# Graph network on one core: the row that VectorE's source one-hots compare with moves from SBUF to PSUM

## The chip, the cores and the metric

One core of a Trainium2 chip runs the whole network as one program. The metric is the device time of one execution in microseconds; the median of three runs before the change is 2574.71 us. The profile is of one further execution on the same kind of core. Its instructions span 2204.9 us.

## The reference, cut to what matters

`x` holds 3125 nodes of 256 features, and there are 53125 edges, sorted by target. Four layers follow each other, each added to `x` after a layer norm: a graph attention, a top-1 mixture of experts, a graph convolution and a top-2 mixture of experts. The change lies in the attention's stage of the edges, and in the counts that the later graph convolution needs:

```
Q, K  = (x @ Wq), (x @ Wk)                        # 8 heads of 32
score = (Q[src] * K[tgt]).sum(-1) * scale + edge_attr @ We
...
out_deg = maximum(segment_sum(ones, src), 1)      # in the second graph layer
msg     = (t1[src] + feat[src] * feat[dst] @ W2) / (sqrt(out_deg[src]) * sqrt(out_deg[dst]))
```

`out_deg`, the number of edges that leave each node, is computed in the stage of the edges, as a by-product: for each tile of 128 edges a product of two one-hots adds to a table of 125 by 25 counts.

## The kernel before

The edges lie as 420 tiles of up to 128 edges, one edge to a partition, in 84 groups of G = 5 tiles. A source node s is written as hi * 125 + lo, with lo in 0..124 and hi in 0..24. The stage of the edges is one block of the program in which every engine runs its own loop over the 84 groups, tied to the others by semaphores only. Its engines do the following for group n, in their own order.

- GpSimd (line 808) issues five gathers, one a tile: 128 rows of `q_rows` in device memory, named by the numbers that `src_t` holds in SBUF, into one of eight buffers of `qr`. It waits until VectorE has freed the buffer of eight groups ago (`s_free`).
- VectorE makes half of the key one-hots of group n+1 (line 978, two instructions). It then waits for `s_ohu` and makes the source one-hots of group n: `oh_lo` (line 1004, 5 x 125 elements a partition) and `oh_hi` (line 1006, 5 x 25), each a compare of a row of numbers with the edges' `lo` or `hi`. The row is `iota_row`, 0..124, in SBUF. It waits for the gathered rows, multiplies them by the expanded keys in PSUM (line 1011, three instructions, `qr` by `psK`) and reduces the products to the dot products (line 1014), which frees the buffer.
- ScalarE makes the other half of the key one-hots (lines 829 and 833), fetches the turned attributes (843, 844) and keeps the scores (854).
- TensorE expands the keys to rows (line 906, 20 matmuls into the three banks of `psK`, each bank once VectorE has freed it), turns the attributes of group n+1 (891), makes the edge scores of group n (918) and adds the counts of group n (line 933, five matmuls into the first 25 columns of `psC`). The counts' bank is opened by a matmul of zeros (877) and read once at the end (1017).
- SyncE loads the local key numbers (764) and the edge attributes (752 to 755).

`s_ohu` counts the groups whose counts TensorE has made. Before the change it starts at GI = 4, so the one-hots of group n wait for the counts of group n-4, the last user of their buffer.

Of the kernel before, what the change touches and what calls it, by code (L numbers as in the profile page):

```python
# [16 lines left out]
P = 125  # L17
T = N_NODES // P
G = 5
NG = T // G  # L20
E = 128
# [5 lines left out]
GI = 4  # L27
# [44 lines left out]
def build(nc, x, src, dst, edge_attr_64, L0_gnn_Wq, L0_gnn_Wk, L0_gnn_Wv, L0_gnn_We, L0_gnn_Wo, L0_gnn_bo,  # L72
# [4 lines left out]
    def sb(ctx, name, shape, dt=F32):  # L77
        return ctx.enter_context(nc.sbuf_tensor(name, shape, dt))
# [4 lines left out]
    def ps(ctx, name, shape, dt=F32):  # L83
        return ctx.enter_context(nc.psum_tensor(name, shape, dt))
# [10 lines left out]
    with top:  # L95
# [22 lines left out]
        iota_row = sb(top, "iota_row", [E, P])  # L118
# [110 lines left out]
        def sem1(name):  # L229
            sems1.append(nc.alloc_semaphore(name=name))  # L230
            return sems1[-1]
# [4 lines left out]
        with ExitStack() as st:  # L236
# [331 lines left out]
            def _(v):  # L568
# [45 lines left out]
                def places():  # L614
# [83 lines left out]
        s_oh, s_ohu, s_cnt, s_webz, s_cntz = (sem1(n) for n in ("onehots_made", "onehots_used", "counts_done", "we_zeroed",  # L698
                                                       "zero_lhs"))
        s_kt, s_kabs, s_kta, s_kx, s_kfree, s_dT, s_dk, s_dst1 = (sem1(n) for n in (  # L700
            "k_onehots", "k_distances", "k_onehots_act", "k_expanded", "k_banks_free", "dots_turned", "dots_kept", "dots_stored"))
        with ExitStack() as st:
# [14 lines left out]
            oh_lo = sb(st, "oh_lo", [E, GI, G, P], BF16)  # L717
            oh_hi = sb(st, "oh_hi", [E, GI, G, T], BF16)
            zb = sb(st, "zb", [P, P], BF16)
            psE = ps(st, "psE1", [128, 2, 512])  # L720
            psS = ps(st, "psS1", [128, 2, 512])
            psC = ps(st, "psC1", [128, 512])
            psK = ps(st, "psK1", [128, 3, 512])
            block = st.enter_context(nc.Block(no_gpsimd_drain=True))
            eav = edge_attr_64[0:FULL * J].rearrange("(p j) f -> p (j f)", p=FULL)
            ear = edge_attr_64[FULL * J:N_EDGES].rearrange("(p j) f -> p (j f)", p=1)
# [145 lines left out]
            @block.tensor  # L872
            def _(pe):
                pe.sem_inc(s_ead, GI)
                pe.sem_inc(s_ohu, GI)
                pe.wait_ge(s_cntz, 1)
                nc.tensor.matmul(psC[0:P, 0:T], zb[:], zb[:, 0:T], start=True, stop=False, skip_group_check=True)
                pe.wait_ge(s_webd, 32)
                def named_bases(i, g):

# [77 lines left out]
                with pe.Fori(begin, EITER - 1) as i:  # L958
# [3 lines left out]
                                 skip_group_check=True).then_inc(s_cnt, 1)  # L962
# [9 lines left out]
            @block.vector  # L972
            def _(v):
                def k_onehots(slot, k_slot, turn):

                    v.wait_ge(s_loc[slot], 16 * (turn + 1))
                    for c in range(CD):
                        last = nc.vector.tensor_scalar(oh_k[:, k_slot, c, :], loc[:, slot, :], k_at[:, c:c + 1], None, ALU.is_equal)
                    last.then_inc(s_kt, 1)

                nc.vector.memset(we2[:], 0.0).then_inc(s_webz, 1)
                nc.vector.memset(ea[:, 0, :], 0.0).then_inc(s_eaz, 1)
                nc.vector.memset(zb[:], 0.0).then_inc(s_cntz, 1)
                nc.vector.memset(ea[:, 1:GI, :], 0.0).then_inc(s_eaz, 1)
                for n in range(2):
                    last = nc.vector.tensor_scalar(part_of[:, n:n + 1], rank_p[:, 0:1], float((n + 1) * R), -float(R), ALU.is_ge, ALU.mult)
                dve_order.link(v, last)
                for n in range(2):
                    dve_order.link(v, nc.vector.tensor_scalar(k_at[:], rank_p[:] if n == 0 else k_at[:], part_of[:, n:n + 1], None, ALU.add))

                dve_order.link(v, nc.vector.tensor_copy(src_f[:], src_i[:]))
                dve_order.link(v, nc.vector.tensor_scalar(lo[:], src_f[:], -float(P // 2), 1.0 / P, ALU.add, ALU.mult))
                dve_order.link(v, nc.vector.tensor_scalar(hi[:], lo[:], MAGIC, None, ALU.add))
                dve_order.link(v, nc.vector.tensor_scalar(hi[:], hi[:], MAGIC, None, ALU.subtract))
                dve_order.link(v, nc.vector.scalar_tensor_tensor(lo[:], hi[:], -float(P), src_f[:], ALU.mult, ALU.add))
                dve_order.link(v, nc.vector.tensor_scalar(k_neg[:], k_at[:], -1.0, None, ALU.mult))
                v.sem_inc(s_kt, GI)
                v.sem_inc(s_kfree, 3)
                k_onehots(0, K_SLOT[0], 0)
                for n in range(NK):  # L1000
                    g, row, at = n % GI, qr[:, n % GQ], slice(n * G, (n + 1) * G)
                    k_onehots((n + 1) % GI, K_SLOT[(n + 1) % GI], (n + 1) // GI)
                    v.wait_ge(s_ohu, n + 1)
                    nc.vector.tensor_tensor(oh_lo[:, g], iota_row[:].unsqueeze(1).to_broadcast([E, G, P]),
                                            lo[:, at].unsqueeze(2).to_broadcast([E, G, P]), ALU.is_equal)
                    nc.vector.tensor_tensor(oh_hi[:, g], iota_row[:, 0:T].unsqueeze(1).to_broadcast([E, G, T]),
                                            hi[:, at].unsqueeze(2).to_broadcast([E, G, T]), ALU.is_equal).then_inc(s_oh, 1)
                    v.wait_ge(s_got[n % GQ], G * 16 * (n // GQ + 1))
                    for m, (a, b) in enumerate(BANKS):
                        v.wait_ge(s_kx, n * 3 + m + 1)  # L1010
                        nc.vector.tensor_tensor(row[:, a:b].rearrange("p u d -> p (u d)"), row[:, a:b].rearrange("p u d -> p (u d)"),  # L1011
                                                psK[:, m, 0:(b - a) * D], ALU.mult).then_inc(s_kfree, 1)
                    v.wait_ge(s_kfree, n * 3 + 6)
                    nc.vector.tensor_reduce(dots[:, :, at].rearrange("p h u -> p u h"),  # L1014
                                            row.rearrange("p u (h d) -> p u h d", h=H), AX.X, ALU.add).then_inc(s_free, 1)
                v.wait_ge(s_cnt, 1)
                dve_order.link(v, nc.vector.tensor_copy(counts[:, 0, :], psC[0:P, 0:T]))

                dve_order.link(v, nc.vector.tensor_scalar(counts[0:1, 0, 0:1], counts[0:1, 0, 0:1], -float(PADS), None, ALU.add))
# [1245 lines left out]
        with ExitStack() as st:  # L2265
# [64 lines left out]
            def _(v):  # L2330
                link = lambda ins: dve_order.link(v, ins)

                def rest(m):

                    _, whole, part = piece(m)
                    v.wait_ge(s_hi7, m + 1)
                    link(nc.vector.tensor_tensor(whole, whole, part[0], ALU.subtract))
                    v.sem_inc(s_rest7, 1)

                def low_part(m):  # L2340

                    _, whole, part = piece(m)
                    v.wait_ge(s_mid7, m + 1)
                    nc.vector.tensor_tensor(part[2], whole, part[1], ALU.subtract).then_inc(s_lo7, 1)
# [56 lines left out]
            def _(act):  # L2401
# [10 lines left out]
                def middle_part(m):  # L2412

                    _, whole, part = piece(m)
                    act.wait_ge(s_rest7, m + 1)
                    nc.scalar.activation(part[1], whole, ACT.Copy).then_inc(s_mid7, 1)
# [69 lines left out]
        with ExitStack() as st:  # L2486
# [24 lines left out]
            psC = ps(st, "psC8", [128, 2, 512])  # L2511
# [382 lines left out]
```

## Time and profile before

| | before |
|---|---|
| median of three runs | 2574.71 us (2570.63 to 2580.15) |
| span of the profiled execution | 2204.9 us |
| median of the runs less that span | 369.8 us |
| TensorE busy | 1760.4 us, 80% |
| VectorE busy | 1277.6 us, 58% |
| GpSimd busy | 1173.9 us, 53% |
| ScalarE busy | 873.7 us, 40% |
| the stage's gathers on GpSimd | from 124.2 to 658 us |

The page gives no time of the profiled execution other than its span; the 369.8 us are the runs' median less the span. Busy time is the sum of an engine's instructions, so a busy share says how full an engine is over the whole program and not what limits a stage. A line of a group has the source line, engine and operation, then what is written and read, the number of instructions, their busy time and the mean of one, and last the time that the engine stood idle just before them, with what ended most of it. "issue" is time of the engine's own in which it waited for nothing that the profile shows. DMA_INDIRECT on GpSimd is the making of a gather's descriptors, not the transfer. In a timeline consecutive instructions of one kind are put together, with their count behind the x.

### The profile page before, as it was taken

Reading aid. Unit: us, or ns where it says so; the run is one execution under the profiler, and the core shown is the slowest. Engines: PE = TensorE matmul, PEld = TensorE weight load, DVE = VectorE, ACT = ScalarE, POOL = GpSimd, SP = SyncE. Lnnn points to the kernel's source line nnn. Section 1 sums busy time; section 2 is a strip of 40 time slices with the busy share of each in tenths; the row PEclk is TensorE's granted clock in tenths of the full one; section 3 lists DMA queues with packets and bytes.
Section 4 is the critical chain, followed back from the end, with each engine's and each line's share of the span. In section 5 each row is a group of like instructions: output and inputs, shape, how many; then the busy total and the mean of one; then the engine's idle time right before and its main releaser. Section 6 shows DMA issues by size and latency. Waiting matters only on the chain. (4 is left out here: it accounts for less than half of the span.)

```text
span 2204.9 us, 38514 instructions
## 1 busy us (share of the span) xinstructions
PE 1760.4 (80%) x11779; PEld 1497.5 (68%) x11780; DVE 1277.6 (58%) x2754; ACT 873.7 (40%) x1797; POOL 1173.9 (53%) x1179
## 2 busy tenths in 40 slices
PE   5737988878775899699708878878778699999996
PEld 4525766666654777588607767666657599999995
DVE  7337977777768633346667788877638722222221
ACT  4425765555553244322142222222225634333332
POOL 2667777777770400056567777777640045444442
PEclk9958987777887899899959898999978699999998
DMA  3588655555565362567567866666650566767775
GB/s 93 137 181 199 169 162 151 154 156 150 157 150 131 79 181 80 140 198 226 181 192 248 263 225 224 222 219 219 214 157 24 181 208 192 203 187 192 199 188 146
DMA packets 203516, 384.67 MB, mean 174 GB/s; under 512 B 43525, under 2 KB 138170, under 8 KB 203199
## 3 DMA queue, kind: packets, MB, share of 16 engines
q1 hardware_dynamic: 136871, 223.77, 33.5%
q0 software_dynamic: 65696, 157.37, 26.8%
q10 hardware_dynamic: 840, 2.16, 0.3%
q8 instruction: 58, 0.95, 0.2%
q14 instruction: 51, 0.42, 0.1%
HBM read 277.93 MB, written 108.69 MB: 175 GB/s over the span
## 5 line engine op out<-in xcount | busy, mean ns | idle before, releaser
L808 POOL DMA_INDIRECT qr<-q_rows,src_t x415 | 407.4, 982 | 126.5 <-issue 124.1
L2303 POOL DMA_INDIRECT fr<-pair_rows,dst_i x381 | 363.0, 953 | 123.6 <-issue 113.1
L2323 PE MATMUL psP<-f_part,onehot 125*128 125x256 bf16 x2925 | 359.8, 286 | 85.2 <-DVE onehot L2349 85.1
L2323 PEld LDWEIGHTS psP<-f_part,onehot 125*128 125x128 bf16 x2925 | 297.2, 103 | 141.2 <-DVE onehot L2349 95.1
L906 PE MATMUL psK<-kp,oh_k 126*128 x1680 | 281.5, 332 | 94.1 <-DVE qr L1011 66.1
L906 PEld LDWEIGHTS psK<-kp,oh_k 126*128 126x128 bf16 x1680 | 191.4, 115 | 164.8 <-issue 99.8
L2361 DVE SCALAR_TENSOR_TENSOR psA<-psA,same,fr 128x256 f32<-128x256 f32 x420 | 206.5, 492 | 75.0 <-DMA fr<-pair_rows,dst_i 42.9
L2443 ACT ACTIVATE acc<-psA 128x1280 f32<-128x1280 f32 x84 | 103.9, 1237 | 331.0 <-DVEq L2364 310.8
L1919 ACT ACTIVATE m1hT<-m1psH,m1par 128x128 f32<-128x128 f32 x448 | 127.7, 368 | 252.7 <-PE m1psH L1939 252.7
L1939 PEld LDWEIGHTS m1psH<-m1xT,n_rows 128*128 128x128 f32 x1792 | 208.7, 192 | 5.0 <-DMA n_rows<-in_L_ffn_W_dram 1.2
L1939 PE MATMUL m1psH<-m1xT,n_rows 128*128 128x128 f32 x1792 | 209.3, 275 | 1.7 <-DMA n_rows<-in_L_ffn_W_dram 1.1
L1962 PE MATMUL m1psY<-w_all,m1hT 128*128 x896 | 203.9, 381 | 0.0
L1011 DVE TENSOR_TENSOR qr<-qr,psK 128x512 f32<-128x512 f32 (+1 forms) x252 | 136.1, 592 | 107.0 <-DMA qr<-q_rows,src_t 103.6
L1884 POOL DMA_INDIRECT sum<-m1yr,to_i x56 | 90.8, 1622 | 190.3 <-DVE m1yr L2024 187.5
L1962 PEld LDWEIGHTS m1psY<-w_all,m1hT 128*128 128x128 f32 x896 | 165.9, 190 | 21.7
L829 ACT ACTIVATE dist<-loc,k_neg 126x640 bf16<-126x640 bf16 x170 | 130.8, 820 | 60.9 <-DMA loc<-locals_ 36.0
L2349 DVE TENSOR_TENSOR onehot<-psP,node_f 125x3200 bf16<-125x3200 f32 x39 | 136.0, 3488 | 4.5 <-PE psP L2314 1.9
L1014 DVE TENSOR_REDUCE dots<-qr 128x40 f32<-128x1280 f32 x84 | 125.0, 1488 | 2.9
L833 ACT ACTIVATE oh_k<-dist,ones 126x1280 bf16<-126x1280 bf16 x85 | 115.8, 1362 | 10.1
L2190 PE MATMUL m0psY<-w_first,m0hT 128*128 x512 | 117.0, 382 | 3.2 <-issue 2.9
L2020 DVE TENSOR_TENSOR m1yr<-m1psY,m1b 128x256 f32<-128x256 f32 x56 | 23.8, 424 | 163.3 <-PE m1psY L1962 163.3
L2190 PEld LDWEIGHTS m0psY<-w_first,m0hT 128*128 128x128 f32 x512 | 94.8, 190 | 18.1 <-issue 6.4
(502 smaller groups left out, 2685.1 us busy)
## 6 DMA issues: line engine op xcount, KB each, us to landing
n_rows<-in_L_ffn_W_dram SPq DMA_DIRECT2D x56, 1024.0 KB
run_rows<-acc SPq DMA_DIRECT2D x84, 640.0 KB
loc<-locals_ SPq DMA_DIRECT2D x85, 157.5 KB
ea<-in_edge_attr_dram SPq DMA_DIRECT2D x84, 140.0 KB
w_first<-in_L_ffn_Wd_dram SPq DMA_DIRECT2D x8, 1024.0 KB, 11.8
w_all<-in_L_ffn_W_dram SPq DMA_DIRECT2D x8, 1024.0 KB, 10.3
m1b<-in_L_ffn_b_dram SPq DMA_DIRECT2D x56, 128.0 KB, 2.9
qr<-q_rows,src_t POOLq DMA_INDIRECT x420
```

Of the source, the lines that this page charges most:

```text
L808: nc.gpsimd.indirect_dma_start(out=qr[:, n % GQ, u, :], out_offset=None, in_=q_rows, in_offset=bass.IndirectOffsetOnAxis(ap=src_t[:, n, u: ...
L829: last = nc.scalar.activation(dist[:, c - CD, :], loc[:, slot, :], ACT.Abs, bias=k_neg[:, c:c + 1])
L906: last = nc.tensor.matmul(psK[:, m, (u - a) * D:(u - a + 1) * D], oh_k[:, K_SLOT[g], c, u * E:(u + 1) * E], kp[:, bass.ds(first[u] + c, 1) ...
L1011: nc.vector.tensor_tensor(row[:, a:b].rearrange("p u d -> p (u d)"), row[:, a:b].rearrange("p u d -> p (u d)"), psK[:, m, 0:(b - a) * D], ...
L1919: last = nc.scalar.activation(hT[s][:, m, :], psH[s][:, m * 128:(m + 1) * 128], ACT.Gelu, bias=par[s][:, m:m + 1] if own_w1 else b1_0[:, m ...
L1939: last = nc.tensor.matmul(psH[s][:, m * 128:(m + 1) * 128], w1[s if own_w1 else 0][:, k, m * 128:(m + 1) * 128], xT[s][:, k, :], start=(k ...
L1962: last = nc.tensor.matmul(psY[:, s, 0:D], hT[s][:, m, :], w, start=(m == 0), stop=(m == KC - 1))
L2190: last = nc.tensor.matmul(psY[:, s, 0:D], hT[s][:, m, :], w2_first[:, bass.ds(first + m, 1), :].rearrange("p a d -> p (a d)"), start=(m == ...
L2303: nc.gpsimd.indirect_dma_start(out=fr[:, n % GI, u, :], out_offset=None, in_=f_rows, in_offset=bass.IndirectOffsetOnAxis(ap=f_at[:, n * G ...
L2323: last = nc.tensor.matmul(psP[:, k % 2, 0:D], onehot[:, k % 2, t, :], f_part[:, c, t, :], start=(t == 0 and c == 0), stop=(t == T - 1 and ...
L2349: nc.vector.tensor_tensor(onehot[:, k % 2], psP[0:P, k % 2, D:D + E].unsqueeze(1).to_broadcast([P, T, E]), node_f[:].unsqueeze(2).to_broad ...
L2361: link(nc.vector.scalar_tensor_tensor(sums(n, u), prev, same[:, n * G + u:n * G + u + 1], fr[:, n % GI, u, :], ALU.mult, ALU.add))
```

## The change

`iota_ps` is a name for columns 128 to 252 of the bank `psC`, whose first 25 columns take the counts. VectorE copies `iota_row` there at the start of the stage, and both source one-hots read it from there. Since TensorE's counts write the same bank, VectorE reads it only between them: `s_ohu` is now raised once by the matmul of zeros (which waits for the copy) and once by the counts of each group, with no head start of four. So the one-hots of group n wait for the counts of group n-1. The counts of group n waited for the one-hots of group n already (`s_oh`).

```diff
+            iota_ps = psC[0:E, 128:128 + P]
...
                 pe.sem_inc(s_ead, GI)
-                pe.sem_inc(s_ohu, GI)
-                pe.wait_ge(s_cntz, 1)
-                nc.tensor.matmul(psC[0:P, 0:T], zb[:], zb[:, 0:T], start=True, stop=False, skip_group_check=True)
+                pe.wait_ge(s_cntz, 2)
+                nc.tensor.matmul(psC[0:P, 0:T], zb[:], zb[:, 0:T], start=True, stop=False, skip_group_check=True)\
+                  .then_inc(s_ohu, 1)
...
                 nc.vector.memset(zb[:], 0.0).then_inc(s_cntz, 1)
+                nc.vector.tensor_copy(iota_ps, iota_row[:]).then_inc(s_cntz, 1)
                 nc.vector.memset(ea[:, 1:GI, :], 0.0).then_inc(s_eaz, 1)
...
                     v.wait_ge(s_ohu, n + 1)
-                    nc.vector.tensor_tensor(oh_lo[:, g], iota_row[:].unsqueeze(1).to_broadcast([E, G, P]),
+                    nc.vector.tensor_tensor(oh_lo[:, g], iota_ps.unsqueeze(1).to_broadcast([E, G, P]),
                                             lo[:, at].unsqueeze(2).to_broadcast([E, G, P]), ALU.is_equal)
-                    nc.vector.tensor_tensor(oh_hi[:, g], iota_row[:, 0:T].unsqueeze(1).to_broadcast([E, G, T]),
+                    nc.vector.tensor_tensor(oh_hi[:, g], iota_ps[:, 0:T].unsqueeze(1).to_broadcast([E, G, T]),
                                             hi[:, at].unsqueeze(2).to_broadcast([E, G, T]), ALU.is_equal).then_inc(s_oh, 1)
```

## Rows read from the trace of the kernel before

**Rows 1.** The page's costliest groups: the stage's gathers.

```profile
L808 POOL DMA_INDIRECT qr<-q_rows,src_t x415 | 407.4, 982 | 126.5 <-issue 124.1
```

**Rows 2.** Busy time by stretch, gathers of line 808: stretch, length, busy (count), clock, DMA.

```profile
124.20:187.90 63.70, 48.71 (x50) 0.61 1.04 216
187.90:280.70 92.80, 71.45 (x70) 0.95 0.63 171
280.70:433.40 152.70, 115.94 (x120) 0.79 0.56 157
433.40:658.00 224.60, 171.34 (x175) 0.80 0.58 154
```

**Rows 3.** The waits from 281 to 658 us: total, times, longest.

```profile
DVE qr L1011 <- DMA qr<-q_rows,src_t: 102.7, 47, 7.2
```

**Rows 4.** Busy time by stretch, all engines: PE, PEld, DVE, ACT, POOL.

```profile
187.90:280.70 92.80, 85.00 (x683) 68.76 (x680) 91.01 (x158) 69.36 (x121) 71.45 (x70) 0.95 0.63 171
280.70:433.40 152.70, 125.99 (x830) 97.60 (x829) 111.72 (x195) 85.66 (x149) 115.94 (x120) 0.79 0.56 157
```

**Rows 5.** Single lines: shortest, median and longest in ns, first and last start.

```profile
L808 POOL DMA_INDIRECT qr<-q_rows,src_t x415: 949/953/1382, 124.2 to 656.9; - x139
...
L2303 POOL DMA_INDIRECT fr<-pair_rows,dst_i x381: 947/953/987, 1105.7 to 1588.4; - x191
...
L1004 DVE TENSOR_TENSOR oh_lo<-iota_row,lo x84: 789/804/809, 139.2 to 659.0; 128x625 bf16<-128x625 f32 x84
...
L1011 DVE TENSOR_TENSOR qr<-qr,psK x252: 406/679/689, 140.1 to 662.0; 128x512 f32<-128x512 f32 x84, 128x256 f32<-128x256 f32 x42
```

**Rows 6.** The timeline from 264.9 to 273.5 us: start, duration, instruction.

```profile
266.06 0.46 PE L933 MATMUL psC<-oh_hi,oh_lo 128*125 128x25 bf16 x5
...
267.21 0.79 DVE L1004 TENSOR_TENSOR oh_lo<-iota_row,lo 128x625 bf16<-128x625 f32 x1
267.46 1.37 POOL L808 DMA_INDIRECT qr<-q_rows,src_t  x1 [0.30 <-issue]
...
271.17 0.67 DVE L978 TENSOR_SCALAR oh_k<-loc,k_at 126x640 bf16<-126x640 bf16 x2
...
271.65 1.01 POOL L808 DMA_INDIRECT qr<-q_rows,src_t  x1 [0.30 <-issue]
271.76 0.80 DVE L1004 TENSOR_TENSOR oh_lo<-iota_row,lo 128x625 bf16<-128x625 f32 x1
...
272.67 1.28 DVE L1011 TENSOR_TENSOR qr<-qr,psK 128x512 f32<-128x512 f32 x2
272.97 0.95 POOL L808 DMA_INDIRECT qr<-q_rows,src_t  x1 [0.30 <-issue]
```

**Rows 7.** The timeline of GpSimd: three of the longer gathers.

```profile
139.44 1.38 POOL L808 DMA_INDIRECT qr<-q_rows,src_t  x1 [0.30 <-issue]
...
355.86 1.11 POOL L808 DMA_INDIRECT qr<-q_rows,src_t  x1 [0.30 <-issue]
...
650.10 1.38 POOL L808 DMA_INDIRECT qr<-q_rows,src_t  x1 [0.30 <-issue]
```

**Rows 8.** The timeline at 1154 us, in the second graph layer.

```profile
1154.08 3.49 DVE L2349 TENSOR_TENSOR onehot<-psP,node_f 125x3200 bf16<-125x3200 f32 x1 [0.15 <-DVE psA L2361]
...
1154.63 0.95 POOL L2303 DMA_INDIRECT fr<-pair_rows,dst_i  x1 [0.31 <-issue]
```

**Rows 9.** The timeline of VectorE at 184.9 us: the reduction of group 3.

```profile
184.94 1.49 DVE L1014 TENSOR_REDUCE dots<-qr 128x40 f32<-128x1280 f32 x1
```

**Rows 10.** The timeline at the stage's start.

```profile
125.68 0.66 PE L891 MATMUL psE<-ident,ea 128*128 128x128 f32 x2 [4.49 <-DMA ea<-in_edge_attr_dram]
...
138.49 0.79 DVE L978 TENSOR_SCALAR oh_k<-loc,k_at 126x640 bf16<-126x640 bf16 x2 [12.21 <-DMA loc<-locals_]
```

**Rows 11.** The timeline at the stage's end.

```profile
660.83 1.61 DVE L1011 TENSOR_TENSOR qr<-qr,psK 128x512 f32<-128x512 f32 x3 [0.88 <-DMA qr<-q_rows,src_t]
...
664.03 1.28 PE L968 MATMUL psK<-ident,dots 127*84 127x127 f32 x5 [3.36 <-DVE dots L1014]
```

## The prediction

> **What bounds the kernel now.** The change touches the stage of the edges only, so I first looked for what sets that stage's length. The stage gathers 420 tiles of query rows, five to a group, 84 groups, and the page has the gathers as GpSimd's costliest group, 0.98 us each with about 0.30 us of issue between them [rows 1]. The table of the gathers by stretch shows them running from 124.2 to 658 us without a hole: 407.43 us in 415 gathers, and the 126.5 us between them [rows 1] make up 534 us, the whole stretch [rows 2]. GpSimd is the chain. The waits of the second part of the stage agree: VectorE waits 102.7 us for gathered rows [rows 3], and before each gather GpSimd has only the 0.30 us of its own issue. VectorE is full only from 187.9 to 280.7 us, 91.0 of 92.8 us, where it works off groups that lay ready [rows 4]; from one group's one-hot to the next it takes 4.55 us there (267.21 to 271.76) [rows 6], about 4.6 in all. From 280.7 us it is 73% busy [rows 4]: GpSimd's five gathers need 5 x (0.95 + 0.30) = 6.3 us, so VectorE has 1.7 us free in each group. So what VectorE or TensorE gains here is worth nothing; only what shortens a gather, or makes GpSimd wait for a free buffer, moves the end.
>
> The gathers are not all alike. Minimum and median are 949 and 953 ns, the longest 1382 [rows 5]. All gathers together are 407.43 - 415 x 0.953 = 11.9 us longer than at the median: that is all that any change to their length can give. By stretch it is 1.1, 4.7, 1.6 and 4.6 us [rows 2]. The timeline says what makes them long. A gather starts at 267.46, in the middle of the source one-hot of line 1004 (267.21 to 268.00), and takes 1.37 us; it ends 0.83 us after the one-hot did [rows 6]. The next pair shows a 1.01 us gather from 271.65, in the middle of the two instructions of line 978 (to 271.84), and it ends 0.82 us after those. It is the same distance, so the same cause: a part of each gather can't go on while such a VectorE instruction runs. I count 19 gathers of 1.37 to 1.38 us, the first at 139.44 and the last at 650.10 [rows 7], and each lies over a one-hot of line 1004 that began 0.24 us before it. They are 2, 10, 0 and 7 in the four stretches, 19 x (1.375 - 0.953) = 8.0 us. The other 3.9 us are some 50 gathers of 0.97 to 1.11 us (the longest in [rows 7]), nearly all behind line 978.
>
> **The change part by part.** Reading the row 0..124 from PSUM changes which memories line 1004 reads: SBUF twice before, SBUF and PSUM after. The trace has two VectorE instructions of just that kind beside gathers. The product of line 1011 reads qr in SBUF and psK in PSUM; a gather that starts inside it (272.97, the product from 272.67) takes 0.95 us [rows 6]. The one-hots of line 2349, the same compare with its row in PSUM, run 3.49 us each, 39 times, beside the gathers of line 2303: one at 1154.63 starts inside such a one-hot and takes 0.95 us [rows 8], and of 381 gathers the longest took 987 ns [rows 5]. So I take the 19 long gathers back to the median: 8.0 us. From below the term is 0 (another cause), from above 11.9 us (if the stall behind line 978 went too; I see no reason, as that instruction isn't changed).
>
> The Trainium skill, "SBUF — State Buffer", section "Who interferes with whom", says two things on this, after the rows above. One is that a VectorE instruction with two SBUF inputs contends with a GpSimd instruction that reads SBUF, which a gather with its row numbers in SBUF does; by that the 8.0 us go. The other, marked there as inferred, is that tensor_tensor did not stall a DMA's descriptors, as they need the write side; by that the sum would be 0. The 1.37 us gathers speak for the first.
>
> What line 978 does afterwards is not in the trace, since VectorE and GpSimd fall into step differently once line 1004 no longer holds a gather up. From 187.9 to 280.7 us the pattern repeats every two groups of VectorE: one gather held 0.42 us by line 1004, one held 0.06 by line 978. With the first gone I take one more short hold for each of the 14 groups of gathers there, 14 x 0.05 = 0.7 us. Bounds: 0, and 84 holds of 0.16 us (the longest such gather has 1.11 us) less the 3.9 there are, 9.5 us.
>
> The duration of the one-hots: from the product's two forms, 406 ns for 256 elements and 679 for 512, I get 799 for the 625 of line 1004, against 804 now [rows 5], and no more than that again for the 125 of line 1006. Between -0.02 and +0.05 us a group, up to 4.2 us of VectorE's time in all, and its 1.7 us of idle time a group hide it; in the full stretch it moves only how soon VectorE catches up. Cost 0.
>
> The catching up itself: the faster gathers put GpSimd 4.2 us further ahead by 280.7 us. VectorE gains 6.3 - 4.6 = 1.7 us a group, so it catches up some three groups later, and nothing is lost. GpSimd must not meet an undrained buffer: group 11's first gather, the 51st, may start once group 3's reduction is done, 184.94 + 1.49 = 186.43 [rows 9]. Fifty start before 187.9 [rows 2], so it has at least 1.5 us of room; two of the 19 holds lie before it, 0.84 us. Over 0.6 us remain, and from there VectorE runs away from it. Cost 0; if the cover fails, some tenths once.
>
> The added wait: the one-hots of group n wait for TensorE's counts of group n-1 instead of n-4. Behind them on VectorE stand the product, which frees TensorE's banks, and the reduction, which frees GpSimd's buffer. In the order of TensorE the counts follow the expansion by turning the attributes and the edge scores; VectorE meanwhile does the last product, the reduction (1.49 us) and line 978 (0.67 us). The tightest of the 83 places is at 266.06 + 0.46 = 266.52 for the counts and 267.21 for the one-hot, 0.69 us [rows 6]. Cost 0, bounds 0 and, should it bite by all of 0.5 us, still under the 1.7 us that are free.
>
> The start: one copy of 125 elements, under the 0.8 us of a one-hot with five times as many [rows 5]. It delays TensorE's zero matmul, after which TensorE waits 4.49 us for a DMA, and a chain of VectorE that then waits 12.21 us for a load [rows 10]. The memset behind the copy lets SyncE issue further attribute loads; SyncE is then still issuing key rows. Cost 0; without the cover, the copy's time once.
>
> The end: VectorE waited 0.88 us for the rows of the last group, at 660.83 [rows 11], so a shift of GpSimd passes through to it. Only of a hold late in the stage no more than 0.88 us would pass, since VectorE is then working off groups that had to wait for three stores of the dots; the last hold, at 650.10, is 0.42 us and passes. Those stores follow VectorE's own progress and move along with it.
>
> **Sum.** -8.0 + 0.7 = -7.3 us. The page gives a span of 2204.9 us; the three runs have a median of 2574.7, 369.8 us more, which lies around the span and is taken as unchanged. 2574.7 - 7.3 = **2567.4 us**, -0.28%.
>
> **The rivals.**
> *More holds in the timed executions than in the profiled one.* How the two engines fall into step decides the number: 10 hits in 14 groups in one stretch, none in 24 in another. For it: nothing pins the phase. Against: the three runs differ by 9.5 us only. At the rate of the second stretch, 60 hits, 25 us would go: 2549.
> *The change doesn't do what it says.* If the cause lies with line 1004 but not with its input (its output or its length), the holds stay: 2574.7. Against: lines 1011 and 2349. (The skill's inferred sentence, given above, would make it this outcome.)
> *Line 978 takes the place.* At its upper bound, +9.5 - 8.0: 2576.2. For it: its holds are the more frequent already; against: each is short, as the instruction is.
> *Slower: the new wait closes a ring.* If the counts came so late, by late attributes or scores, that VectorE stood over 1.7 us in each group, GpSimd would wait for buffers. At 2.0 us it costs 84 x 0.3 = 25 us: 2600. Against: 0.69 us of room at the tightest place, and VectorE has no wait for counts anywhere.
>
> **How the numbers follow.** Forecast 0.58; more holds 0.14; no effect 0.16; line 978 0.07; the ring 0.05. About 0.5%, 12.9 us, is what a measurement can tell from no change. So faster 0.14, same 0.58 + 0.16 + 0.07 = 0.81, slower 0.05. The runs before spread over 9.5 us, so I put 3 us of measurement beyond no effect, 2578 above, and reach halfway into the first rival below, 2556. The forecast's own range is 2562 to 2572.
>
> **What would show it.** In the profile after, line 808 has no gather over 1.2 us and a mean near 0.963 (395.5 + 4.6 = 400.1 us in 415), and its last start comes 7 us earlier, at 650. Lines 1004 and 1006 last 0.80 and 0.27 us. VectorE has no wait for counts. The stage's end (line 968's transposes, 664.03 now [rows 11]) moves to 657, and everything behind it by the same. Wrong would be: gathers of 1.37 us over line 1004 still (no effect), a sum of line 808 that hardly falls with more gathers of 1.0 to 1.1 us (line 978), idle time of VectorE ahead of line 1004 (the ring), or a stage end that doesn't follow the gathers.

## The result and the profile after

The changed kernel takes 2616.85 us (median of four runs, 2607.91 to 2625.97) and the kernel before takes 2572.67 us (four runs, 2568.96 to 2580.15). The ratio is 1.0155, 95% interval 1.012 to 1.019: slower by 1.5%, or 44.2 us between the medians. The forecast of 2567.4 us, its range up to 2578 and the likeliest case, a change of less than 0.5%, are all wrong. A ratio leaves out runs that lie over 1.5% above the fastest of their kernel, which matters below for one kernel only, the wait alone on the first long chip, where four of eight lie so.

| | before, as profiled | after, as profiled |
|---|---|---|
| span of the profiled execution | 2204.9 us | 2618.9 us |
| time of that execution | not given | 2620.63 us |
| median of the runs | 2572.67 us | 2616.85 us |

Every run made here took its span and some 1.7 us more. So all but 1.7 of the 369.8 us lie inside the execution, and not around its span. The profile that the prediction read is of an execution of some 2206.6 us (estimate: 2204.9 + 1.7), and the timed runs are from a kind of chip on which the same kernel takes a sixth longer. The runs below met both kinds. Each chip was used for one set of runs only, so a lasting property of a chip can't be told from a condition that it was in at the time; "kind" means here no more than the time that was measured. On four chips the kernel before took 2206.9 to 2212.3 us; I call them the short chips. On two others it took 2578.0 and 2578.2 us; these are the long chips, and the result above belongs with them. The profiles before and after must therefore not be laid beside each other; the partner of the profile after is that of the kernel before on a long chip, though it need not be the same chip.

The page after:

```profile
span 2618.9 us, 38514 instructions
...
L809 POOL DMA_INDIRECT qr<-q_rows,src_t x415 | 395.4, 953 | 334.2 <-DVE dots L1016 216.3
L2305 POOL DMA_INDIRECT fr<-pair_rows,dst_i x381 | 364.1, 956 | 273.0 <-DVEq L2367 155.1
...
L1013 DVE TENSOR_TENSOR qr<-qr,psK 128x512 f32<-128x512 f32 (+1 forms) x252 | 135.9, 590 | 202.8 <-remote 197.1
...
L1006 DVE TENSOR_TENSOR oh_lo<-psC,lo 128x625 bf16<-128x625 f32 x84 | 67.5, 804 | 158.3 <-remote 154.8
```

And the page of the kernel before on a long chip (the run that I call before-long, one of 2578 us):

```profile
span 2577.8 us, 38514 instructions
...
L808 POOL DMA_INDIRECT qr<-q_rows,src_t x415 | 416.1, 1003 | 278.4 <-DVE dots L1014 161.8
```

Against [rows 1] the gathers are all at the median, 953 ns: the change did to them what was forecast. But GpSimd now waits for buffers: 216.3 us for VectorE's reduction, and 161.8 already before the change. On a long chip GpSimd is not the chain. VectorE waits ahead of the one-hots (154.8 us) and of the product (197.1). "remote" means that at the release no instruction of this trace ended: where a case is followed below, the matmuls that it waited for were long done.

The waits of the profile after, 200 to 820 us (engine, line, releaser: total, times, longest), where [rows 3] had VectorE wait for gathered rows:

```profile
POOL qr L809 <- DVE dots L1016: 195.5, 35, 5.7
DVE qr L1013 <- remote: 165.7, 35, 7.7
PE psC L934 <- issue: 144.8, 94, 4.5
DVE oh_lo L1006 <- remote: 129.1, 33, 5.9
```

The end of the stage, which answers to the last of [rows 11], in before-long and after:

```profile
852.62 1.06 PE L968 MATMUL psK<-ident,dots 127*84 127x127 f32 x8 [1.50 <-DVE dots L1014]
```

```profile
893.16 1.92 PE L969 MATMUL psK<-ident,dots 127*84 127x127 f32 x8 [1.84 <-DVE dots L1016]
```

That is 40.5 us later; the spans differ by 41.1. In these two profiles all of the loss arises in the edge stage. Its start is about the same: the first recorded gather is at 126.8 in the one and 124.6 in the other.

### The profile page after: what moved, and what is told of

Same layout as the page of the kernel before. It is cut to its first block and busy times, and to the rows that moved or that the text cites. A ratio compares the mean times of both kernels' runs of the same rounds, so it can differ in the third digit from the quotient of the medians.

```text
span 2618.9 us, 38514 instructions
## 1 busy us (share of the span) xinstructions
PE 1854.3 (71%) x11779; PEld 1531.9 (58%) x11780; DVE 1278.3 (49%) x2755; ACT 875.9 (33%) x1797; POOL 1162.3 (44%) x1179
## 5 line engine op out<-in xcount | busy, mean ns | idle before, releaser
L809 POOL DMA_INDIRECT qr<-q_rows,src_t x415 | 395.4, 953 | 334.2 <-DVE dots L1016 216.3
L2325 PE MATMUL psP<-f_part,onehot 125*128 125x256 bf16 x2925 | 423.3, 302 | 165.2 <-issue 145.4
L2325 PEld LDWEIGHTS psP<-f_part,onehot 125*128 125x128 bf16 x2925 | 307.5, 107 | 275.9 <-issue 197.9
L907 PEld LDWEIGHTS psK<-kp,oh_k 126*128 126x128 bf16 x1680 | 198.3, 120 | 216.7 <-issue 161.1
L1013 DVE TENSOR_TENSOR qr<-qr,psK 128x512 f32<-128x512 f32 (+1 forms) x252 | 135.9, 590 | 202.8 <-remote 197.1
L934 PE MATMUL psC<-oh_hi,oh_lo 128*125 128x25 bf16 x420 | 52.6, 220 | 164.5 <-issue 148.2
L855 ACT ACTIVATE score<-psS 128x40 f32 (+1 forms) x84 | 20.2, 240 | 404.6 <-remote 315.3
L1006 DVE TENSOR_TENSOR oh_lo<-psC,lo 128x625 bf16<-128x625 f32 x84 | 67.5, 804 | 158.3 <-remote 154.8
L934 PEld LDWEIGHTS psC<-oh_hi,oh_lo 128*125 128x125 bf16 x420 | 43.0, 162 | 152.9 <-issue 133.9
```

What stands on the lines that cost most here:

```text
L809: nc.gpsimd.indirect_dma_start(out=qr[:, n % GQ, u, :], out_offset=None, in_=q_rows, in_offset=bass.IndirectOffsetOnAxis(ap=src_t[:, n, u: ...
L907: last = nc.tensor.matmul(psK[:, m, (u - a) * D:(u - a + 1) * D], oh_k[:, K_SLOT[g], c, u * E:(u + 1) * E], kp[:, bass.ds(first[u] + c, 1) ...
L2325: last = nc.tensor.matmul(psP[:, k % 2, 0:D], onehot[:, k % 2, t, :], f_part[:, c, t, :], start=(t == 0 and c == 0), stop=(t == T - 1 and ...
```

## The experiments

Short chips first, in the order of the questions. Ratios are to the kernel before on the same chip, with 95% intervals; "SBUF row" means that the one-hots read `iota_row` as before.

**The changed kernel again.**

> The changed kernel itself, beside the kernel before, which takes 2210 us in the runs beside the last four kernels and 2573 us in the runs that the prediction went by. There reading PSUM without a wait gave 2200.5 against 2209.3 us, and the wait alone nothing (2211.0 against 2210.0). Theory C (the 44 us belong to the condition in which before takes 2573 us): beside a before of 2210 us it takes 2201 to 2205 us, ratio 0.996 to 0.998; beside a before of 2573, 2617. Theory D (the wait and the PSUM row together cost 44 us in any condition): ratio 1.02.

Measured: 2203.68 us against 2211.6, ratio 0.9964 (0.9952 to 0.9976). That is -7.9 us where I had forecast -7.3. By stretch, as [rows 2]:

```profile
124.20:187.90 63.70, 46.62 (x49) 0.61 1.03 216
187.90:280.70 92.80, 69.97 (x74) 0.96 0.66 179
280.70:433.40 152.70, 115.83 (x122) 0.83 0.59 157
433.40:658.00 224.60, 166.49 (x173) 0.79 0.59 153
```

398.9 us in 415 gathers (a gather on a border counts in both stretches), where I had forecast 400.1. Its single lines, to be held against [rows 5]:

```profile
L809 POOL DMA_INDIRECT qr<-q_rows,src_t x415: 947/953/1138, 126.7 to 651.3; - x139
...
L1006 DVE TENSOR_TENSOR oh_lo<-psC,lo x84: 787/800/806, 142.3 to 655.9; 128x625 bf16<-128x625 f32 x84
...
L1008 DVE TENSOR_TENSOR oh_hi<-psC,hi x84: 269/276/281, 143.1 to 656.7; 128x125 bf16<-128x125 f32 x84
```

No gather over 1.14 us, the one-hots 0.80 and 0.28 us, and no wait for counts. The holds are gone and not merely missed: 28 gathers start inside a compare of line 1006 and take 0.949 to 0.962 us. In the profile of before 24 start inside one of line 1004, and 19 of them take 1.37 us or more. The kernel before, built again, on another short chip, has 25 such holds:

```profile
L808 POOL DMA_INDIRECT qr<-q_rows,src_t x415: 949/953/1617, 124.3 to 659.4; - x139
```

**The added wait alone**, SBUF row.

```diff
-                pe.sem_inc(s_ohu, GI)
+                pe.sem_inc(s_ohu, 1)
```

> The added wait alone: the row stays in SBUF, and the one-hots of group n wait for the counts of group n-1. Theory A (the wait costs: in typical executions the counts come late, and VectorE stands for them): slower by all or most of the 44 us, ratio 1.012 to 1.018. Theory B (the memory that the row is read from costs, or what it changes on GpSimd): ratio 0.998 to 1.002. If both have a part: between.

Measured 2211.02 us, ratio 1.001 (0.9995 to 1.0026). Twice more on other short chips:

> The added wait alone, again, for a chip on which before takes 2573 us. Theory E (there the late signals hold VectorE at the added wait, and the two one-hots behind it, 0.80 + 0.28 us, come onto the path in each of the 37 to 40 places where it stood): 40 x 1.08 = 43 us slower, ratio 1.017. Theory B (the memory): ratio 1.00. Beside a before of 2210 us: ratio 1.00, as measured.

> The added wait alone, for a chip on which before takes 2573 us: 2617 there by theory E, 2573 by theory B. Beside a before of 2210 us: ratio 1.00 again.

0.9995 (0.9981 to 1.0009) and 1.0003 (0.9985 to 1.0021). The wait is free there. The kernel before against itself, as the measure of what such a comparison can tell:

> The kernel before, unchanged, for a second profile. The first one spans 2204.9 us while its runs take 2573; after's profile spans 2618.9 and its run takes 2620.6. If the first profile was of an unusually short execution, this one spans some 2570 us and shows the gathers of line 808 stretched over far more than 534 us, with VectorE and TensorE waiting as they do after the change; if profiling itself shortens this kernel by 370 us, it spans 2205 again. Ratio to before 1.00 either way.

> The kernel before once more, on whatever chip this lands. On the chips of the two calls before it took 2210 us, in the runs that the prediction was held against 2573. If it takes 2573 here, its profile will say where the 363 us go; I expect then what the changed kernel's profile of 2618.9 us shows: VectorE and ScalarE waiting for TensorE's signals that come microseconds after the matmuls are done. If it takes 2210 again it only repeats.

> The kernel before, for its profile on a chip where it takes 2573 us, should this be one. There I expect TensorE's signals to come microseconds late in both gather stages. Else 2210 again.

1.0006 (0.9988 to 1.0024), 0.9998 (0.9985 to 1.0011), 1.0016 (1.0 to 1.0032).

**The row alone.** The counts' five matmuls are left out (the later layer's degrees are then not computed), once with the SBUF row and once with the PSUM row, both with the head start of four.

```diff
-                    for u in range(G):
-                        last = nc.tensor.matmul(psC[0:P, 0:T], oh_lo[:, g, u, :], oh_hi[:, g, u, :], ...)
-                    last.then_inc(s_ohu, 1)
+                    pe.sem_inc(s_ohu, 1)
```

> The counts' five matmuls a group are left out (the table of counts stays zero), the row stays in SBUF, head start of four as before. A base for the next run. TensorE has 0.46 us a group less to do. If TensorE's counts lie on the path of typical executions, faster than before by up to 84 x 0.46 = 39 us (ratio 0.985); if not, ratio 1.00.

> The counts' matmuls left out as in the run beside it, the row read from PSUM, and the head start of four kept, which is free of a clash since TensorE writes nothing to that bank in the loop. Theory A: the same time as the run beside it, or up to 12 us faster, since no gather is held up. Theory B: slower than the run beside it by all or most of 44 us.

2209.32 us, 1.0003 (0.9986 to 1.0021), and 2200.52 us, 0.995 (0.9934 to 0.9967): 8.8 us between them. Their gathers, SBUF row first:

```profile
L808 POOL DMA_INDIRECT qr<-q_rows,src_t x415: 949/953/1414, 126.1 to 658.7; - x139
```

```profile
L809 POOL DMA_INDIRECT qr<-q_rows,src_t x415: 949/955/1128, 124.2 to 651.2; - x139
```

The two differ in the row's memory and the copy that puts it there at the start. With the SBUF row 19 gathers take over 1.2 us, with the PSUM row none, though 22 start inside the compare. That the source of line 1004's row makes the long holds is shown.

**The one-hots behind the product**, otherwise the changed kernel: the counts of a group come one group later, and the wait stands behind the product and the reduction of its own group. It still stands ahead of the next group's product, with the one-hots and line 978 between them, since VectorE works in the order of its program. So the expectation's words that nothing which frees a bank or a buffer stands behind the wait any more hold for the same group only.

```diff
-                    v.wait_ge(s_ohu, n + 1)
-                    nc.vector.tensor_tensor(oh_lo[:, g], iota_ps ...)      # and oh_hi
...
                     nc.vector.tensor_reduce(...)
+                    v.wait_ge(s_ohu, n + 1)
+                    nc.vector.tensor_tensor(oh_lo[:, g], iota_ps ...)      # and oh_hi
```

> The changed kernel, with the one-hots of group n and their wait moved behind the product and the reduction of group n, and TensorE's counts moved one group later. Nothing that frees a bank or a buffer stands behind the wait any more. Beside a before of 2210 us: as the changed kernel, 2203, plus up to 1 us for one-hots at the end. Beside a before of 2573: theory E says it loses the 44 us, at or under 2573; theory B says 2617.

2202.67 us, 0.996 (0.9946 to 0.9975): as the changed kernel.

**What a late signal costs.** The signal that frees the one-hots is raised later, with the edge scores of the next group; SBUF row. Near: distance one, as in the change. Far: distance four, as before.

```diff
-                pe.sem_inc(s_ohu, GI)          # near; far has GI - 1 here
...
-                    last.then_inc(s_ohu, 1)    # in the counts
...
+                        if n == 1: last.then_inc(s_ohu, 1)     # in the edge scores
```

> The row in SBUF as before, no read of PSUM. The one-hots of group n wait for the counts of group n-1, and the signal for those counts is raised late, only with TensorE's edge scores of group n, behind the expansion of group n. So the added wait, with a signal late by one expansion (2.1 to 4.0 us). Theory E (late signals make the wait cost): the ring one-hots 1.08, product 0.68, expansion 2.1 to 4.0, attributes and scores 1.35 to 1.95, is 5.2 to 7.7 us a group against GpSimd's 6.3; slower by 20 to 80 us. If VectorE's idle time hides a late signal too: no change.

> The same late signal, but with the old distance of four groups: the one-hots of group n wait for the signal of group n-4. Under every theory no change, ratio 1.00; it shows that the late signal alone is free.

Near: 2282.78 us against 2206.89, 1.0346 (1.0316 to 1.0375), +76 us. Some 13 of them go with longer gathers: 57 take over 1.2 us here and 21 in the kernel before on that chip, 22.0 and 9.0 us over the median. Far: 2209.79, 1.0012 (0.9996 to 1.0028). The waits of the near one, 200 to 820 us:

```profile
POOL qr L808 <- DVE dots L1014: 18.3, 16, 1.2
...
DVE oh_lo L1004 <- PE psS L917: 172.5, 78, 5.1
```

So on the same chip distance one is free with a prompt signal and costly with a late one, and distance four takes the late one up.

**On long chips: the pieces again.** The first gives the partner profile used above.

> The kernel before, for its profile where it takes 2573 us. Else 2210 us and nothing new.

> The added wait alone. On a chip where before takes 2573 us: 2617 if the wait carries the 44 us (theory E), 2573 if the memory does (theory B). Beside a before of 2210 us: ratio 1.00.

> The row in PSUM without any near wait, the counts left out. On a chip where before takes 2573 us: at or under 2573 by theory E, 2617 by theory B. Beside a before of 2210 us: 2201, as measured.

The kernel before: 2583.82 us against 2578.2, 1.0009 (0.9977 to 1.0042). The wait alone: median 2609.48 us of eight runs from 2577.45 to 2627.48; its ratio of 1.0042 (0.9993 to 1.009) can't decide. In its profile, of a run of 2602.20 us, the stage ends 20.7 us later than in before-long. The row without counts: 2589.67 us, 1.0024 (0.9998 to 1.0051), so nothing is gained there, although the 38 gathers over 1.2 us of before-long are gone. The same without counts and with the SBUF row was not run on a long chip. Last, the three versions with the near wait, on the other long chip:

> The added wait alone. On the chip where before takes 2578 us its eight runs went from 2577 to 2627 with a median of 2609; there again 2595 to 2615, which would put some 30 of the 44 us on the wait. Elsewhere as before.

> The changed kernel. On the chip where before takes 2578 us: 2617 again. Elsewhere 8 us under before.

> The changed kernel with the one-hots and their wait behind product and reduction. On the chip where before takes 2578 us: theory E (one-hots behind a late signal, ahead of the product) says the loss goes, 2570 to 2590; if it is the near wait wherever it stands, 2605 to 2620. Elsewhere 2202 again.

| on the second long chip (before 2578.04) | us | ratio | stage's last transposes start | GpSimd waits for buffers |
|---|---|---|---|---|
| wait alone | 2610.11 | 1.0101 (1.0053 to 1.0149) | 892.10 | 209.1 us in 38 |
| changed kernel | 2619.15 | 1.0145 (1.0106 to 1.0184) | 887.50 | 210.3 in 38 |
| one-hots behind the product | 2612.02 | 1.0133 (1.0093 to 1.0172) | 888.37 | 211.3 in 38 |
| for comparison, first long chip: before | 2583.82 | 1.0009 | 852.62 | 161.8 in 39 |
| the wait alone there | 2609.48 | 1.0042 (0.9993 to 1.009) | 873.27 | 186.8 in 38 |
| and the row without counts | 2589.67 | 1.0024 | 861.48 | 188.0 in 38 |

On the second long chip the wait alone, with the row in SBUF and some long gathers still there, ends the stage as late as the whole change does; in the profile from the first it has half of that loss:

```profile
L808 POOL DMA_INDIRECT qr<-q_rows,src_t x415: 947/954/1567, 125.6 to 855.2; - x139
...
  DVE dots L1014: 209.1, 38
```

Its waits, 200 to 820 us, and under them those of the version with the one-hots behind the product:

```profile
DVE qr L1011 <- remote: 157.6, 33, 7.6
...
DVE oh_lo L1004 <- remote: 124.2, 30, 9.4
```

```profile
DVE qr L1010 <- remote: 175.5, 36, 8.2
...
DVE oh_lo L1016 <- remote: 115.1, 32, 5.6
```

My theory for that version was that the wait hurts because one-hots and product of its own group stand behind it. Moved, the kernel is as slow (1.0133 for 1.0145, with intervals that overlap), so its place within the group isn't the reason. That the wait hurts by holding up the next product isn't tested by it: that product still stands behind it.

## Where the 41 us come from

On a long chip GpSimd works two groups at a time: ten gathers, then a wait until a reduction frees the next buffer. One such turn of before-long and the start of the next, GpSimd and then VectorE (start, duration, instruction, idle time before it in brackets):

```profile
415.46 0.95 POOL L808 DMA_INDIRECT qr<-q_rows,src_t  x1 [3.75 <-DVE dots L1014]
...
427.27 0.96 POOL L808 DMA_INDIRECT qr<-q_rows,src_t  x1 [0.30 <-issue]
432.12 0.95 POOL L808 DMA_INDIRECT qr<-q_rows,src_t  x1 [3.90 <-DVE dots L1014]
```

```profile
422.02 0.69 DVE L1011 TENSOR_TENSOR qr<-qr,psK 128x512 f32<-128x512 f32 x1 [0.72 <-PE psK L906]
427.03 0.69 DVE L1011 TENSOR_TENSOR qr<-qr,psK 128x512 f32<-128x512 f32 x1 [4.33 <-remote]
429.91 0.42 DVE L1011 TENSOR_TENSOR qr<-qr,psK 128x256 f32<-128x256 f32 x1 [2.19 <-PE psK L906]
430.37 1.49 DVE L1014 TENSOR_REDUCE dots<-qr 128x40 f32<-128x1280 f32 x1
```

While the ten gathers are issued (415.46 to 428.2), a signal of TensorE's reaches VectorE only every 4 to 5 us. Two products of the group get theirs within the burst; the third product and the reduction follow it, and GpSimd goes on at 432.12. The same in the profile after:

```profile
400.94 0.95 POOL L809 DMA_INDIRECT qr<-q_rows,src_t  x1 [5.57 <-DVE dots L1016]
...
412.25 0.95 POOL L809 DMA_INDIRECT qr<-q_rows,src_t  x1 [0.31 <-issue]
418.78 0.95 POOL L809 DMA_INDIRECT qr<-q_rows,src_t  x1 [5.57 <-DVE dots L1016]
```

```profile
409.53 0.81 DVE L1006 TENSOR_TENSOR oh_lo<-psC,lo 128x625 bf16<-128x625 f32 x1 [3.68 <-remote]
...
415.37 1.62 DVE L1013 TENSOR_TENSOR qr<-qr,psK 128x512 f32<-128x512 f32 x3 [4.84 <-remote]
417.02 1.49 DVE L1016 TENSOR_REDUCE dots<-qr 128x40 f32<-128x1280 f32 x1
```

Now a wait in the burst goes to the one-hots (3.68 us), and all three products of the group, 1.62 us, come behind the burst's end at 413.2. Their counts' matmuls were done: the last five before it ran at 404.77 for 0.41 us, 4.3 us before the one-hot could begin.

```profile
404.77 0.41 PE L934 MATMUL psC<-oh_hi,oh_lo 128*125 128x25 bf16 x5
405.03 2.34 PE L907 MATMUL psK<-kp,oh_k 126*128 x20
```

By the traces' semaphore records the signal of these counts rose at 409.50, and the one-hot began at 409.53. The products' signals are no better: the expansion that they wait for ended at 407.4, and its three signals rose between 415.28 and 415.43.

The period of two groups is 432.12 - 415.46 = 16.66 us before and 418.78 - 400.94 = 17.84 us after: 1.18 us more, although ten gathers without a hold are shorter. The two are typical: over the stage the median period is 16.7 and 17.9 us, and 17.3 and 17.9 for the wait alone on the first and the second long chip. With 38 such waits for a buffer 1.18 us would make some 45 us, against 40.5 measured at the stage's end. The account of GpSimd fits better: its gathers take 20.7 us less (416.1 to 395.4), its waits for a buffer 54.5 us more (161.8 to 216.3), and from first to last gather it needs 35.7 us more (692.7 to 728.4). So the long gathers went as forecast, and the wait took back more than that.

From the same records I took how long after the end of a group's last count the semaphore next rose, as a median: 0.014 us in the profile of before and in the changed kernel on a short chip; 3.1 us in the profile after, 3.6 in the wait alone on the second long chip and 5.1 in before-long. Some rises are missing from the records, so the long medians are rough and rather too high. The signals are late there with either kernel. Before, distance four took it up, and VectorE has no wait ahead of line 1004 in before-long, as in the far experiment; after, many are waited for, as in the near one.

The second graph layer's gathers, whose code isn't changed, are slowed on a long chip too: GpSimd waits 149.6 us there in before-long,

```profile
L2303 POOL DMA_INDIRECT fr<-pair_rows,dst_i x381: 951/957/1072, 1313.3 to 1949.5; - x191
...
  DVEq L2365: 149.6, 27
```

and its gathers take from first to last 636.2 us where the profile of before had 482.7 [rows 5]. With the 160 us of the edge stage (692.7 for 532.7 from first to last gather) that is 314 of the 372.9 us between the two spans.

What stays open: why signals come late on some chips, or in some condition of theirs, while GpSimd issues gathers; no run changes that. It is a thing of the gathers' stages by the records: in before-long the median from the end of an instruction of TensorE to the next rise of its semaphore is 0.014 us away from gathers, and 3.2 and 3.1 us beside those of the edge stage and the second graph layer (rough, as above). On the second long chip the changed kernel's median is 9 us above that of the wait alone, though its stage ends no later; the intervals overlap, so it can't be told from none. Whether the PSUM row costs something of its own on a long chip is therefore not settled. That the row without counts waits 188.0 us for buffers, and not 161.8, isn't explained either; it fits that its gathers without holds reach the next wait sooner, but that is argued, not shown.

## Why the prediction was wrong, step by step

- **Which engine is the chain**: GpSimd. Right for the execution in the profile and the other short chips. On the long chip it waits 161.8 us for buffers already before the change, and shorter gathers brought nothing there (1.0024).
- **The long gathers are holds by line 1004, -8.0 us**: right. They go with the row's move to PSUM, with counts or without, -7.9 and -8.8 us on short chips. "The change doesn't do what it says" is refuted. The Trainium skill, "SBUF — State Buffer", section "Who interferes with whom", reports of a probe that tensor_tensor did not stall a DMA, and marks as inferred the reason, that making descriptors needs the write side only. The gathers of 1.37 us over line 1004 [rows 6], and their end once one input lies in PSUM, speak against that for this gather; the section's rule that two SBUF inputs contend with a GpSimd instruction that reads SBUF agrees with both.
- **Line 978 takes 0.7 us of it**: too much. 398.9 - 415 x 0.953 = 3.4 us are above the median, 3.9 before; the term has the wrong sign and is small.
- **The one-hots' duration, the start, the catching up, 0 each**: right, 0.800 us where 0.799 was forecast, and no new wait.
- **The end passes the gain on**: right on a short chip. The last gather starts at 651.3 for 656.9, and the transposes at 660.04 for 664.03, though the first gather came 2.5 us later; in the rebuilt kernel before they start at 667.00.
- **The added wait, cost 0, bounds 0**: the step that failed. It is so on short chips (1.001, 0.9995, 1.0003), where the signal comes 0.014 us after the matmul. On the long ones, where the signal comes 3 to 5 us late, it alone costs 31 and 32 us between medians (1.0042, which doesn't decide, and 1.0101, 14 to 38 us), and puts off the stage's end by half or all of what the whole change does. I took the end of the counts' matmul for the moment of the signal and measured 0.69 us of room from it; the rows showed that room for one execution on a short chip. The slower rival named the mechanism, VectorE held so long by counts that GpSimd waits for buffers, and priced it at 2600 us with a chance of 0.05. Its wait came true: VectorE stands 154.8 us ahead of the one-hots after the change, 1.8 us a group. Its reason did not. The attributes and scores weren't late, the signal was, and the 1.7 us of idle time a group had been read on a short chip.
- **"369.8 us lie around the span and are taken as unchanged"**: the step from which the other failure comes. The gap was no overhead: around a span lie 1.7 us. Read as what it was, a sign that the timed runs were in a regime that the profile doesn't show, it would have forbidden bounds of 0 on a wait with 0.69 us of measured room and moved much weight to the ring, and it would have taken weight from any gain on GpSimd.

No version here is best everywhere: the changed kernel and the one with the one-hots behind the product on short chips (2203.7 and 2202.7 us), the kernel before on long ones. A version with the row in PSUM and the old distance of four, counts kept, was not tried: the counts write the bank that the one-hots would read.

## What to carry to other kernels

Before any sum, compare the profile's span with the timed runs. Here they belong together within 2 us; a gap beyond what the runs scatter by means that the profile is of another regime, and every slack read from it is good for that regime only. A wait at a distance of one group is worth its risk only if the signal's own delay is known; the distance of four groups hid several microseconds of it for nothing. A compare of VectorE with two SBUF inputs holds up a gather that starts inside it, and moving one input to PSUM ended that, but it paid only where GpSimd was the chain.

## What the runs showed of the hardware

The same program takes 2207 to 2212 us on four chips and 2578 on two, each met once, at a mean granted clock of 0.88 (0.878 to 0.880 in the four profiles of the kernel before) against 0.82 (0.815) of full speed. Whether the clock is a cause or follows from TensorE standing idle isn't settled; the 20 matmuls of an expansion take 2.34 us at their shortest on a long chip too. The difference lies mostly in the two gather stages, and the signal of TensorE's counts rises 3 to 5 us late there while GpSimd issues gathers, against 0.014 us.
